# A five-stage gather kernel in which SyncE relays nothing: GpSimd waits for TensorE's count by a constant, VectorE for the landing of a fixed group

## The chip, the cores and the metric

The kernel runs on one core of a Trainium2 chip. The metric is the time of one execution on the device, in microseconds: before the change the median of three runs is 7366.6 us (7364.74 to 7367.6).

## What is computed

Four graph layers are applied to 6250 nodes of 256 features over 100,000 edges (`src`, `dst`; sorted by `dst`), each followed by a residual and a layer norm. What matters here is the sum over the edges that end in a node:

```
agg = jax.ops.segment_sum(h[src], dst, num_segments=n)              # layer 0
gathered = support[edge_col] * edge_val[:, None]                    # layer 1
out = jax.ops.segment_sum(msg, dst, num_segments=n_nodes)           # layer 2, three times
msg = jax.nn.relu(x[src] + edge_attr)                               # layer 3
agg = jax.ops.segment_sum(msg, dst, num_segments=x.shape[0])
```

The kernel does five of these sums by gathering rows by `src` and adding them up per `dst`: its gather stages 0 (layer 0), 2, 3, 4 (layer 2) and 5 (layer 3). Layer 1 is done in another way (a scatter with addition, between stages 0 and 2).

## The kernel before

**Blocks, tiles, pairs.** The sorted edges are cut into 782 blocks of 128, the nodes into 49 tiles of 128. A pair is a block and a tile that share an edge; there are about 830, padded to 832. Since both are sorted, pair p of tile t belongs to block p - t. Pairs are worked in 208 batches of four, blocks are gathered in 196 groups of four.

**A gather stage, engine by engine.**
- GpSimd (`gather`, line 466) issues one indirect DMA for each block: it brings the 128 source rows into one of the 64 slots of the buffer `ring`. The landing of group k is counted on the semaphore `gathered{k % 16}`. From group 16 on a group may start only when slots are free.
- VectorE (`one_hots`, line 1123) makes, for batch q, four 128 x 128 matrices that say which edge of the block ends in which node of the tile. Two batches fit the buffer `onehot`. It waits for the rows of the batch's last block, for the accumulator of its last tile (`cleared`), and for the first matmul of the batch before (`summed`).
- TensorE (`sum_pairs`, line 608) multiplies, four matmuls a batch, into one of four accumulators, and counts each pair on `summed{n}`. The count starts at 1.
- ScalarE (`sum_tiles`, line 870) takes a finished tile out of its accumulator.
- SyncE stands between them (`relay`). For each group it waits for the landing, adds the number of blocks to `landed{n}` (line 256), reads from the table `need` the last pair that uses group k - 4 (line 249), waits until `summed{n}` has reached it, and adds 1 to `freed` (line 251). GpSimd waits for `freed` before group k, which stands for group k - 16. So slots become free exactly when their last pair is done. VectorE waits for `landed{n}` against a number that it reads from the table `lasts`: exactly the last block that the batch uses.
- Stage 5 differs: GpSimd waits there for `summed5` against the constant `(k + 1) * BATCH - SLOTS + T`, and VectorE adds edge features to each landed group (`messages`, lines 1133 and 1134) right ahead of the one-hots of the batch with the same number.

**What else runs beside stage 0.** SyncE's relay of stage 0 also loads the tiles of `x` for a first matrix product (`y_step`), ten groups ahead of their use. VectorE compares shifted edge lists (`rows_of_edges`, lines 1218 and 1219) after each of the one-hots 1 to 127. Stage 0 starts before the tables of pairs are ready: GpSimd fills the ring, then waits.

Every engine works its own instructions in program order; a wait holds back all that stands behind it on that engine. After a stage all nodes must be summed before the next table can be written and the next stage's gathers can start.

Of the kernel before, what the change touches and what calls it, by code (L numbers as in the profile page):

```python
# [5 lines left out]
P = 128  # L6
ALU = mybir.AluOpType
ACT = mybir.ActivationFunctionType
ET = mybir.EngineType
# [6 lines left out]
BATCH = 4  # L16
SLOTS = 64
GROUPS = SLOTS // BATCH
ONEHOTS = 8
EAS = 8  # L20
BEHIND = 4
ZG = 13
Y0 = 40
YS = 2
# [8 lines left out]
def gnn_kernel(nc, a, out):  # L33
    N, D = a["x"].shape
    E = a["src"].shape[0]
    T = -(-N // P)
    LAST = N - (T - 1) * P
    NP = T * P
    DH = D // P
    W = D + 1  # L40
    B = -(-E // P)
# [3 lines left out]
    PAIRS = -(-(B + T) // (2 * BATCH)) * (2 * BATCH)  # L45
    HALF = PAIRS // 2
    QB = PAIRS // BATCH
    GB = -(-B // BATCH)
# [12 lines left out]
    with ExitStack() as ctx:  # L61
# [5 lines left out]
        def sm(name):  # L67
            if name not in sems:
                sems[name] = ctx.enter_context(nc.semaphore(name))
            return sems[name]  # L70
# [12 lines left out]
        lasts = {"dst": sb("lasts_dst", [1, QB * 2], U16)}  # L83
        need = {"dst": sb("need_dst", [1, 2 * P], U16)}
# [96 lines left out]
        y_rows_in = [bias[:, i, :] for i in range(3)] + [wt[w_][:, i, :] for w_ in "bd" for i in range(DH)]  # L181
        YB = len(y_rows_in)
        y_turned_in = [wt["c"][:, i, :] for i in range(DH)]

        def y_step(q, lag):
            t, r = divmod(q - Y0 - lag, YS)
            return t if r == 0 and 0 <= t < T else None
# [13 lines left out]
        def landing(n, k):  # L201

            n -= n > 1
            size = lambda kk: min(BATCH, B - kk * BATCH)
            g = k % GROUPS
            each = sum(size(kk) for kk in range(g, GB, GROUPS))
            return sm(f"gathered{g}"), 16 * (n * each + sum(size(kk) for kk in range(g, k + 1, GROUPS)))
# [6 lines left out]
        def before_stage(n):  # L214

            return n - (n > 1)
# [6 lines left out]
        def _(sp):  # L223
            def load(dst, src, sem):
                sp.dma_start(dst, src).then_inc(sem, 16)
# [17 lines left out]
            def weights(k, name):  # L243
                load(wt[k][:, :, :], a[name].rearrange("(h k) n -> k h n", k=P), sm("weights_in"))

            def free_slots(n, k):

                if 0 <= k < GB - GROUPS:
                    last_pair = sp.value_load(need[AGGS[n][0]][0:1, k:k + 1], min_val=1, max_val=PAIRS + 1)
                    sp.wait_ge(sm(f"summed{n}"), last_pair)  # L250
                    sp.sem_inc(sm("freed"), 1)

            def relay(n):
                for k in range(GB):
                    sp.wait_ge(*landing(n, k))
                    sp.sem_inc(sm(f"landed{n}"), min(BATCH, B - k * BATCH))
                    if k == BEHIND and n == 0:
                        sp.wait_ge(sm("tables_done"), n + 1)
                    free_slots(n, k - BEHIND)
                    t = y_step(k, -10) if n == 0 else None  # L260
                    if t is not None:
                        if t >= YB:
                            sp.wait_ge(sm("y_turned"), t - YB + 1)
                        elif t == 3 + DH:
                            sp.wait_ge(sm("w_turned"), 1)
                        if t >= 3:
                            sp.wait_ge(sm(f"x_in{t % 3}"), 16 * (t // 3))
                        rows_ = min(P, N - t * P)
                        load(y_rows_in[t % YB][0:rows_, :], a["x"][t * P:t * P + rows_, :], sm(f"x_in{t % 3}"))

            def store_table(name, src, ready, base=0):
                for t in range(T):
# [29 lines left out]
            for i, name in enumerate(("b1", "g1", "beta1", "br", "b2", "g2", "beta2")):  # L302
                columns(i, "L0_gnn_" + name)
            load(wt["d"][:, :, :], a["L0_gnn_w1"].rearrange("(h o) k -> o h k", o=P), sm("wnat_in"))
            relay(0)
            sp.wait_ge(sm("summed0"), PAIRS + 1)
            sp.wait_ge(sm("xr_free"), 1)
            for q, name in enumerate(("L0_gnn_w1", "L0_gnn_wr", "L0_gnn_wroot", "L0_gnn_w2")):
# [31 lines left out]
                    load(part[:, g % 2, j, 0:(t1 - t0) * D],  # L340
                         sums[j][0:NP, :].rearrange("(p t) d -> p (t d)", t=T)[:, t0 * D:t1 * D], sm(f"sums_in{g % 2}"))
            store_table("g0", lambda t: tile(H, t), sm("ln1_own"))
            relay(2)
            store_table("g1", lambda t: tile(H, t), sm("gcn_rows"))
            relay(3)
            store_table("g2", lambda t: tile(H, t), sm("gcn_rows"), T)
            sp.wait_ge(sm("gcn_rows"), 2 * T)
            for q, name in enumerate(("L3_gnn_W1", "L3_gnn_W2")):
# [2 lines left out]
                columns(i, "L3_gnn_" + name)  # L351
            for i, name in enumerate(("bn2_gamma", "bn2_beta", "bn2_mean", "bn2_var", "b2")):
                row(E1[:, i * D:(i + 1) * D], "L3_gnn_" + name, sm("bn2_in"))
            relay(4)
            store_table("x3", lambda t: tile(X, t), sm("ln2_rows"))

            disorder = sp.value_load(unsorted[0:1, 0:1], min_val=0, max_val=E)
# [27 lines left out]
        def _(pool):  # L385
# [61 lines left out]
            def gather(n, features=False):  # L447
                which, name = AGGS[n]
                if n > 2:
                    pool.wait_ge(sm(f"summed{n - 1}"), PAIRS + 1)  # L450
                for k in range(GB):
                    if k >= GROUPS:
                        if n < 5:
                            pool.wait_ge(sm("freed"), before_stage(n) * (GB - GROUPS) + k - GROUPS + 1)
                        else:
                            pool.wait_ge(sm(f"summed{n}"), (k + 1) * BATCH - SLOTS + T)
                    here = range(k * BATCH, min(B, (k + 1) * BATCH))
                    if features:
                        if k >= 2:
                            pool.wait_ge(sm("landed5"), (k - 1) * BATCH)  # L460
                        for b in here:
                            pool.indirect_dma_start(
                                out=EA[:, b % EAS, :], out_offset=None, in_=a["edge_attr_256"][:, :],
                                in_offset=bass.IndirectOffsetOnAxis(ap=eid[:, b:b + 1], axis=0)).then_inc(sm(f"ea_in{k % 2}"), 16)
                    for b in here:
                        pool.indirect_dma_start(  # L466
                            out=ring_v[:, b % SLOTS, 0:D], out_offset=None, in_=table[name][:, :],
                            in_offset=bass.IndirectOffsetOnAxis(ap=idx_ap[which][:, b:b + 1], axis=0))\
                            .then_inc(landing(n, k)[0], 16)
# [523 lines left out]
        def _(dve):  # L993
# [114 lines left out]
            def one_hots(n, q):  # L1108

                which = AGGS[n][0]  # L1110
                _, (block_end, tile_end_) = nc.values_load_multi_w_load_instructions(
                    lasts[which][0:1, 2 * q:2 * q + 2], engines=[ET.DVE], min_val=0, max_val=1023,
                    skip_runtime_bounds_check_because="made of clamped numbers")
                if q >= 2:
                    dve.wait_ge(sm(f"summed{n}"), (q - 1) * BATCH + 1)
                elif n > 2:
                    dve.wait_ge(sm(f"summed{n - 1}"), PAIRS + 1)
                elif n == 2:
                    dve.wait_ge(sm("c_mm"), QB)
                s = q * BATCH % ONEHOTS  # L1120
                dve.wait_ge(sm(f"landed{n}"), block_end)
                dve.wait_ge(sm(f"cleared{n}"), tile_end_)  # L1122
                last = tt(onehot[:, s:s + BATCH, :], iota_row[:, :].unsqueeze(1).to_broadcast((P, BATCH, P)),  # L1123
                          dl_ap[which][:, q * BATCH:(q + 1) * BATCH].unsqueeze(2).to_broadcast((P, BATCH, P)), ALU.is_equal)
                last.then_inc(sm("onehot_ready"), 1)
# [158 lines left out]
            for i in range(T + 2):  # L1284
# [4 lines left out]
                if i >= 2:  # L1289
                    t = i - 2  # L1290
# [237 lines left out]
```

## Time and profile before

| | |
|---|---|
| timed runs, median | 7366.6 us |
| profiled execution, span | 8074.1 us |
| TensorE matmul busy | 4409.3 us (55%) |
| VectorE busy | 2662.5 us (33%) |
| GpSimd busy | 5199.4 us (64%) |
| ScalarE busy | 866.9 us (11%) |
| indirect gathers | 3910 (782 a stage), 0.946 us each at the median |

The page is of one execution with the profiler on. Its span runs from the first to the last instruction, and the page records no time around it; it is 707.5 us longer than the median of the timed runs. "Busy" of GpSimd is here the issue of indirect DMAs. In the page's wait lists a releaser "remote" is one that the profile could not name, and "issue" is time in which an engine waited for nothing that the profile shows.

### The profile page before, as it was taken

Reading aid. Unit: us, or ns where it says so; the run is one execution under the profiler, and the core shown is the slowest. Engines: PE = TensorE matmul, PEld = TensorE weight load, DVE = VectorE, ACT = ScalarE, POOL = GpSimd, SP = SyncE. Lnnn points to the kernel's source line nnn. Section 1 sums busy time; section 2 is a strip of 40 time slices with the busy share of each in tenths; the row PEclk is TensorE's granted clock in tenths of the full one; section 3 lists DMA queues with packets and bytes.
Section 4 is the critical chain, followed back from the end, with each engine's and each line's share of the span. In section 5 each row is a group of like instructions: output and inputs, shape, how many; then the busy total and the mean of one; then the engine's idle time right before and its main releaser. Section 6 shows DMA issues by size and latency. Waiting matters only on the chain.

```text
span 8074.1 us, 63990 instructions
## 1 busy us (share of the span) xinstructions
PE 4409.3 (55%) x16498; PEld 3303.5 (41%) x16498; DVE 2662.5 (33%) x5948; ACT 866.9 (11%) x2041; POOL 5199.4 (64%) x4804
## 2 busy tenths in 40 slices
PE   3455559866666651444445444445544545556557
PEld 2344338755444440333334333334333334334336
DVE  5443212655555544111112111112111114544445
ACT  0000002322322220000002000002000001000002
POOL 4776660188888883666663666663666663677774
PEclk9777779988888875777777677667777667766768
DMA  2333334166666665333332333333333333666662
GB/s 64 95 104 103 97 90 136 19 72 71 72 72 72 71 72 177 89 91 94 91 94 86 87 93 93 92 93 94 88 93 93 92 91 101 185 182 185 184 182 64
DMA packets 497711, 811.01 MB, mean 100 GB/s; under 512 B 97410, under 2 KB 367636, under 8 KB 497364
## 3 DMA queue, kind: packets, MB, share of 16 engines
q0 software_dynamic: 300288, 615.29, 34.2%
q1 hardware_dynamic: 197076, 191.58, 7.4%
q8 instruction: 159, 2.61, 0.1%
q14 instruction: 188, 1.54, 0.1%
HBM read 652.63 MB, written 153.86 MB: 100 GB/s over the span
## 4 chain that ended last, share of the span: by engine, by line
another core or an unknown queue 28%; PE 25%; POOL 20%; issue 17%; DVE 6%; DMA 2%; DVEq 1%; SPq 0%; ACT 0%; POOLq 0%; ACTq 0%
PE acc L608 17%; POOL sums_by_src L488 11%; POOL ring L466 9%; DVE onehot L1123 3%; PE acc L532 3%; PE acc L527 2%; PE high L527 1%; DVEq L1122 1%; DVE X L1154 1%; PE high L518 1%; DMA ring<-table_x,idx_dst 1%; DMA sums_by_src<-ring,E 1%; PE high L532 1%; PE acc L518 0%
## 5 line engine op out<-in xcount | busy, mean ns | idle before, releaser
L608 PE MATMUL acc<-ring,onehot 128*128 x8320 | 2738.6, 490 | 2828.7 <-DVE onehot L1123 1780.1
L608 PEld LDWEIGHTS acc<-ring,onehot 128*128 128x128 f32 x8320 | 1958.4, 246 | 3581.4 <-issue 3237.5
L466 POOL DMA_INDIRECT ring<-table_g,idx_dst x2346 | 2290.3, 976 | 1338.0 <-issue 683.5
L1123 DVE TENSOR_TENSOR onehot<-iota_row,dl_dst 128x512 f32<-128x512 f32 x1040 | 720.3, 694 | 3556.4 <-remote 2262.8
L488 POOL DMA_INDIRECT sums_by_src<-ring,E x782 | 1208.1, 1545 | 613.0 <-ACT high L925 373.9
L466 POOL DMA_INDIRECT ring<-table_x,idx_dst x782 | 833.1, 1065 | 418.8 <-issue 343.1
L466 POOL DMA_INDIRECT ring<-in_x_dram,idx_dst x782 | 792.2, 1013 | 407.8 <-issue 243.3
L768 PE MATMUL high<-H,ring 128*128 x1664 | 546.1, 485 | 455.3 <-ACT high L925 441.6
L768 PEld LDWEIGHTS high<-H,ring 128*128 128x128 f32 x1664 | 375.3, 236 | 550.7 <-issue 490.0
L870 ACT COPY H<-acc 128x256 f32<-128x256 f32 x196 | 72.9, 372 | 4461.8 <-PE acc L608 2781.7
L1365 DVE TENSOR_SCALAR ring<-acc,E 128x128 f32<-128x128 f32 x832 | 283.7, 402 | 575.9 <-PE acc L536 575.9
L1133 DVE TENSOR_TENSOR ring<-ring,E 128x1024 f32<-128x1024 f32 x196 | 239.8, 1223 | 507.3 <-DMA ring<-table_x,idx_dst 476.9
L939 ACT COPY ring<-high 128x512 f32<-128x512 f32 x392 | 210.4, 589 | 1005.6 <-DMA sums_by_src<-ring,E 979.0
L536 PEld LDWEIGHTS acc<-ring,onehot 128*128 128x128 f32 x1664 | 240.0, 207 | 137.7 <-issue 133.6
L536 PE MATMUL acc<-ring,ones 128*128 128x512 f32 x416 | 271.8, 742 | 2.3 <-DVE ring L1353 2.3
L1353 DVE TENSOR_SCALAR ring<-ident,E,ones 128x128 f32<-128x128 f32 x832 | 244.2, 386 | 0.0
L1361 DVE TENSOR_SCALAR onehot<-iota_row,dl_dst,ones 128x128 f32<-128x128 f32 x832 | 234.2, 355 | 0.0
L536 PE MATMUL acc<-ring,onehot 128*128 128x128 f32 x1664 | 232.1, 285 | 2.4 <-DVE ring L1365 2.4
L925 ACT ACTIVATE high<-ones 128x512 f32<-128x512 f32 x396 | 221.1, 591 | 6.2
L527 PE MATMUL high<-wt_c,wt_a 128*128 128x128 f32 x392 | 72.1, 343 | 189.0 <-issue 189.0
L527 PEld LDWEIGHTS high<-wt_c,wt_a 128*128 128x128 f32 x392 | 66.4, 249 | 202.0 <-issue 200.2
L1134 DVE TENSOR_SCALAR ring<-ring 128x1024 f32<-128x1024 f32 x196 | 136.0, 694 | 21.2 <-DVE ring L1133 0.5
(259 smaller groups left out, 2914.9 us busy)
## 6 DMA issues: line engine op xcount, KB each, us to landing
E<-in_edge_attr_dram SPq DMA_DIRECT2D x781, 128.0 KB
ring<-table_g,idx_dst POOLq DMA_INDIRECT x2346
table_g<-H SPq DMA_DIRECT2D x147, 128.0 KB, 1.7
ring<-sums_by_src SPq DMA_DIRECT2D x36, 512.0 KB, 4.8
sums_by_src<-ring SPq DMA_DIRECT2D x2, 6272.0 KB, 38.8
ring<-in_x_dram,idx_dst POOLq DMA_INDIRECT x782
sums_by_src<-ring,E POOLq DMA_INDIRECT x782, 3.8
ring<-table_x,idx_dst POOLq DMA_INDIRECT x782
```

The lines of the kernel that those rows point to most:

```text
L466: pool.indirect_dma_start(out=ring_v[:, b % SLOTS, 0:D], out_offset=None, in_=table[name][:, :], in_offset=bass.IndirectOffsetOnAxis(ap=id ...
L488: pool.indirect_dma_start(out=sums[j][:, :], out_offset=bass.IndirectOffsetOnAxis(ap=to_b[:, b:b + 1], axis=0), in_=rows[:, b % (4 * BATCH ...
L527: last = pe.matmul(chunk(to, o), wk, val, start=(i == 0), stop=(i == len(steps) - 1))
L532: last = pe.matmul(to[:, 0:D], chunk(val, k), wk[:, k, :], start=(k == 0), stop=(k == DH - 1))
L536: return pe.matmul(to, w_, v, start=start, stop=stop, skip_group_check=True)
L608: pe.matmul(acc4[:, ds(to, width)], onehot[:, (q * BATCH + j) % ONEHOTS, :], ring[:, ds(slot, width)], start=False, stop=True, skip_group_ ...
L768: last = pe.matmul(high[:, ds(to, D)], cT[:, (k * BATCH + j) % ONEHOTS, :], H[:, ds(at, D)], start=False, stop=True, skip_group_check=True)
L1123: last = tt(onehot[:, s:s + BATCH, :], iota_row[:, :].unsqueeze(1).to_broadcast((P, BATCH, P)), dl_ap[which][:, q * BATCH:(q + 1) * BATCH] ...
L1133: link(tt(g, g, EA[:, at:at + here, :], ALU.add))
L1353: last = ts(diag[:, p % ONEHOTS, :], ident[:, :], src_q[:, p:p + 1], ones[:, 0:1], ALU.mult, ALU.mult)
L1361: ts(onehot[:, p % ONEHOTS, :], iota_row[:, :], dl["dst"][:, p:p + 1], ones[:, 0:1], ALU.is_equal, ALU.mult)
L1365: last = ts(eqw[:, p % ONEHOTS, :], bank[k % 2][:, j * P:(j + 1) * P], src_q[:, p:p + 1], w_q[:, p:p + 1], ALU.is_equal, ALU.mult)
```

## The change

SyncE's `relay` and `free_slots` are gone from all stages. In stage 0 SyncE only loads the tiles of `x`, one after another, as their buffers come free. GpSimd waits in stages 0, 2, 3 and 4 as it does in stage 5: for TensorE's own count, against a constant. VectorE waits for its batch q in those stages for the landing of the whole group q (none for batches 196 to 207, since there is no such group), and reads one number from its table instead of two. Stage 5 stays as it was.

```
-            def free_slots(n, k):
-                if 0 <= k < GB - GROUPS:
-                    last_pair = sp.value_load(need[AGGS[n][0]][0:1, k:k + 1], min_val=1, max_val=PAIRS + 1)
-                    sp.wait_ge(sm(f"summed{n}"), last_pair)
-                    sp.sem_inc(sm("freed"), 1)
-
-            def relay(n):
-                for k in range(GB):
-                    sp.wait_ge(*landing(n, k))
-                    sp.sem_inc(sm(f"landed{n}"), min(BATCH, B - k * BATCH))
-                    if k == BEHIND and n == 0:
-                        sp.wait_ge(sm("tables_done"), n + 1)
-                    free_slots(n, k - BEHIND)
-                    t = y_step(k, -10) if n == 0 else None
-                    if t is not None:
...
+            def x_for_first_pass():
+                for t in range(T):
+                    if t >= YB:
+                        sp.wait_ge(sm("y_turned"), t - YB + 1)
+                    elif t == 3 + DH:
+                        sp.wait_ge(sm("w_turned"), 1)
+                    if t >= 3:
+                        sp.wait_ge(sm(f"x_in{t % 3}"), 16 * (t // 3))
...
-            relay(0)
+            x_for_first_pass()
...
-            relay(2)
...
-            relay(3)
...
-            relay(4)
...
                     if k >= GROUPS:
-                        if n < 5:
-                            pool.wait_ge(sm("freed"), before_stage(n) * (GB - GROUPS) + k - GROUPS + 1)
-                        else:
-                            pool.wait_ge(sm(f"summed{n}"), (k + 1) * BATCH - SLOTS + T)
+                        pool.wait_ge(sm(f"summed{n}"), (k + 1) * BATCH - SLOTS + T)
...
-                _, (block_end, tile_end_) = nc.values_load_multi_w_load_instructions(
-                    lasts[which][0:1, 2 * q:2 * q + 2], engines=[ET.DVE], min_val=0, max_val=1023,
+                first_word = 2 * q if n == 5 else 2 * q + 1
+                _, ends = nc.values_load_multi_w_load_instructions(
+                    lasts[which][0:1, first_word:2 * q + 2], engines=[ET.DVE], min_val=0, max_val=1023,
...
-                dve.wait_ge(sm(f"landed{n}"), block_end)
-                dve.wait_ge(sm(f"cleared{n}"), tile_end_)
+                if n == 5:
+                    dve.wait_ge(sm("landed5"), ends[0])
+                elif q < GB:
+                    dve.wait_ge(*landing(n, q))
+                dve.wait_ge(sm(f"cleared{n}"), ends[-1])
```

No instruction of GpSimd, VectorE or TensorE moves past another; what changes is what they wait for. On GpSimd, at the start of stage 0, the rows of before and then of the changed kernel (the 64 gathers that fill the ring, then group 16 and the first gather of group 17; `freed` is SyncE's count, `summed0` TensorE's):

```order
L466 DMA ring<-in_x_dram,idx_dst 128x256 [waits edges_ready,idx_ready]
L466 DMA ring<-in_x_dram,idx_dst 128x256 x63
L466 DMA ring<-in_x_dram,idx_dst 128x256 [waits freed]
L466 DMA ring<-in_x_dram,idx_dst 128x256 x3
L466 DMA ring<-in_x_dram,idx_dst 128x256 [waits freed]
```

```order
L445 DMA ring<-in_x_dram,idx_dst 128x256 [waits edges_ready,idx_ready]
L445 DMA ring<-in_x_dram,idx_dst 128x256 x63
L445 DMA ring<-in_x_dram,idx_dst 128x256 [waits summed0]
L445 DMA ring<-in_x_dram,idx_dst 128x256 x3
L445 DMA ring<-in_x_dram,idx_dst 128x256 [waits summed0]
```

The gathers stand where they stood; the wait for `freed` has become one for `summed0`, for group 16 for the value 17 * 4 - 64 + 49 = 53.

On VectorE, near the end of stage 2, batches 193 to 195 of before and then 193 to 197 of the changed kernel (`gathered1` to `gathered3` are the landings of groups 193 to 195):

```order
L1123 TENSOR_TENSOR onehot<-iota_row,dl_dst 128x512 [waits cleared2,landed2,summed2]
L1111 TENSOR_LOAD lasts_dst
L1123 TENSOR_TENSOR onehot<-iota_row,dl_dst 128x512 [waits cleared2,landed2,summed2]
L1111 TENSOR_LOAD lasts_dst
L1123 TENSOR_TENSOR onehot<-iota_row,dl_dst 128x512 [waits cleared2,landed2,summed2]
```

```order
L1106 TENSOR_TENSOR onehot<-iota_row,dl_dst 128x512 [waits cleared2,gathered1,summed2]
L1091 TENSOR_LOAD lasts_dst
L1106 TENSOR_TENSOR onehot<-iota_row,dl_dst 128x512 [waits cleared2,gathered2,summed2]
L1091 TENSOR_LOAD lasts_dst
L1106 TENSOR_TENSOR onehot<-iota_row,dl_dst 128x512 [waits cleared2,gathered3,summed2]
L1091 TENSOR_LOAD lasts_dst
L1106 TENSOR_TENSOR onehot<-iota_row,dl_dst 128x512 [waits cleared2,summed2]
L1091 TENSOR_LOAD lasts_dst
L1106 TENSOR_TENSOR onehot<-iota_row,dl_dst 128x512 [waits cleared2,summed2]
```

The wait for SyncE's `landed2` has become one for the landing of the group with the batch's own number, and from batch 196 on (the last two rows) there is none.

## Rows read from the trace of the kernel before

**Rows 1.** The page: span, busy time of each engine, the costliest gather group.
```profile
span 8074.1 us, 63990 instructions
PE 4409.3 (55%) x16498; PEld 3303.5 (41%) x16498; DVE 2662.5 (33%) x5948; ACT 866.9 (11%) x2041; POOL 5199.4 (64%) x4804
L466 POOL DMA_INDIRECT ring<-table_g,idx_dst x2346 | 2290.3, 976 | 1338.0 <-issue 683.5
```
**Rows 2.** Windows of the gather instructions, first to last, stages 0, 2 and 5.
```profile
core 0: us, POOL busy (x), PEclk, DMA share, GB/s
19.90:1204.60 1184.70, 792.20 (x782) 0.79 0.32 92
3130.80:4243.00 1112.20, 765.76 (x782) 0.70 0.32 92
...
6773.80:7905.90 1132.10, 833.13 (x782) 0.68 0.63 181
```
**Rows 3.** Timeline of VectorE, start of stage 2.
```profile
3137.59 0.69 DVE L1123 TENSOR_TENSOR onehot<-iota_row,dl_dst 128x512 f32<-128x512 f32 x1 [8.94 <-SPq L256]
3142.54 0.69 DVE L1123 TENSOR_TENSOR onehot<-iota_row,dl_dst 128x512 f32<-128x512 f32 x1 [4.26 <-issue]
...
3187.31 0.69 DVE L1123 TENSOR_TENSOR onehot<-iota_row,dl_dst 128x512 f32<-128x512 f32 x1 [21.06 <-remote]
3209.01 0.69 DVE L1123 TENSOR_TENSOR onehot<-iota_row,dl_dst 128x512 f32<-128x512 f32 x1 [21.01 <-remote]
```
**Rows 4.** Timeline of GpSimd, start of stage 2: last gather of group 0.
```profile
3134.70 0.95 POOL L466 DMA_INDIRECT ring<-table_g,idx_dst  x1 [0.30 <-issue]
```
**Rows 5.** SyncE's instructions of line 249, 3160 to 3235 us, then 166 to 215.
```profile
L249 SPq FUSED_REGOPS  x6: 691/701/717, 3164.1 to 3216.7; - x6
...
L249 SPq FUSED_REGOPS  x14: 147/147/147, 166.6 to 212.7; - x14
```
**Rows 6.** Timeline of TensorE, 3186 to 3232 us.
```profile
3188.15 3.78 PE L608 MATMUL acc<-ring,onehot 128*128 x8 [18.22 <-DVE onehot L1123]
```
**Rows 7.** GpSimd's waits: stage 2, then stage 5.
```profile
POOL ring L466 <- SPq L251: 118.2, 37, 12.9
...
POOL ring L466 <- remote: 48.4, 29, 3.2
POOL ring L466 <- PE acc L608: 27.3, 19, 21.7
```
**Rows 8.** Windows of the one-hots, from last gather's end to last matmul.
```profile
1204.60:1237.40 32.80, 8.28 (x12) 1.00 0.02 5
4243.00:4281.20 38.20, 9.68 (x14) 0.98 0.02 4
...
7905.90:7943.40 37.50, 9.67 (x14) 0.98 0.02 6
```
**Rows 9.** Timeline of VectorE, end of stage 2.
```profile
4258.32 0.69 DVE L1123 TENSOR_TENSOR onehot<-iota_row,dl_dst 128x512 f32<-128x512 f32 x1 [1.85 <-PE acc L608]
...
4276.13 0.69 DVE L1123 TENSOR_TENSOR onehot<-iota_row,dl_dst 128x512 f32<-128x512 f32 x1 [1.99 <-PE acc L608]
```
**Rows 10.** Timeline of TensorE, end of stage 2.
```profile
4253.75 1.99 PE L608 MATMUL acc<-ring,onehot 128*128 x8 [0.52 <-issue]
```
**Rows 11.** Timeline of GpSimd, start of stage 0.
```profile
166.40 1.65 POOL L466 DMA_INDIRECT ring<-in_x_dram,idx_dst  x1 [66.60 <-SPq L251]
...
204.99 1.65 POOL L466 DMA_INDIRECT ring<-in_x_dram,idx_dst  x1 [0.30 <-issue]
```
**Rows 12.** Timeline of VectorE, start of stage 0.
```profile
163.24 0.69 DVE L1123 TENSOR_TENSOR onehot<-iota_row,dl_dst 128x512 f32<-128x512 f32 x1 [6.09 <-ACT acc L887]
...
201.47 1.01 DVE L1219 TENSOR_TENSOR H<-H 128x819 f32<-128x819 f32 x1
203.18 0.69 DVE L1123 TENSOR_TENSOR onehot<-iota_row,dl_dst 128x512 f32<-128x512 f32 x1 [0.69 <-PE acc L608]
```
**Rows 13.** Timeline of TensorE beside it.
```profile
204.02 2.00 PE L608 MATMUL acc<-ring,onehot 128*128 x8 [1.35 <-DVE onehot L1123]
```

More of the change, by code:

```diff
@@ L20 @@
 EAS = 8
-BEHIND = 4
 ZG = 13
@@ L244, in weights @@
                 load(wt[k][:, :, :], a[name].rearrange("(h k) n -> k h n", k=P), sm("weights_in"))
-            def free_slots(n, k):
-                if 0 <= k < GB - GROUPS:
-                    last_pair = sp.value_load(need[AGGS[n][0]][0:1, k:k + 1], min_val=1, max_val=PAIRS + 1)
-                    sp.wait_ge(sm(f"summed{n}"), last_pair)
-                    sp.sem_inc(sm("freed"), 1)
-            def relay(n):
-                for k in range(GB):
-                    sp.wait_ge(*landing(n, k))
-                    sp.sem_inc(sm(f"landed{n}"), min(BATCH, B - k * BATCH))
-                    if k == BEHIND and n == 0:
-                        sp.wait_ge(sm("tables_done"), n + 1)
-                    free_slots(n, k - BEHIND)
-                    t = y_step(k, -10) if n == 0 else None
-                    if t is not None:
[L262 to L269, printed above, removed]
+            def x_for_first_pass():
[6 more added lines that the diff above has]
+                        sp.wait_ge(sm(f"x_in{t % 3}"), 16 * (t // 3))
+                    rows_ = min(P, N - t * P)
+                    load(y_rows_in[t % YB][0:rows_, :], a["x"][t * P:t * P + rows_, :], sm(f"x_in{t % 3}"))
             def store_table(name, src, ready, base=0):
```

## The prediction

> **What bounds the kernel now.** I read the page first, then the windows of the five gather stages, then the timelines at the start and the end of a stage, and last the waits. The page shows no engine near full: GpSimd 64%, TensorE 55% [rows 1]. So the bound has to be read stage by stage. In the windows of the gather instructions each stage lasts 1110 to 1185 us and GpSimd issues 782 gathers in it [rows 2]. At the start of stage 2, before anything is late, the gathers take 0.95 us and 0.30 us of issue lie between two [rows 4], so a gather costs 1.25 us and a group of four 5.0 us, and VectorE makes one batch of one-hots every 4.95 us (3137.59, 3142.54), right after each landing [rows 3]. There GpSimd's issue is the bound and the others follow. A batch costs TensorE 1.99 us and 0.52 us between two [rows 10], 2.51 us, when nothing is missing: half of what a group costs GpSimd.
>
> Twenty microseconds later the picture is another one. One-hots come every 21.7 us [rows 3], a batch of eight matmul records that the trace models with 3.78 us is followed by 18 us of nothing [rows 6], and SyncE's small register instruction takes 0.701 us where it takes 0.147 us elsewhere [rows 5]. The consumers fall behind until the ring is full, and GpSimd waits 118.2 us in stage 2 for slots [rows 7]. The question on which the forecast hangs is whether the timed runs have these stretches. The profiled span is 8074.1 us [rows 1], the median of the timed runs 7366.6 us: 707.5 us less. Take the stretches away and the stages at 782 x 1.25 = 977 us each: stages 2, 3, 4 (3 and 4 are like 2, within 2 us) and 5 lose 3 x 134 + 155 = 557 us [rows 2]; stage 0 runs from 166.4 us [rows 11] to 1204.6 with 718 gathers, 898 us, and is left with 140, of which (792.2 / 782 - 0.95) x 782 = 49 us is longer gathers that may stay, so it loses 91; and the ends of stage, 33 to 38 us [rows 8], shrink in the four stages before the last to about 6 (below), 4 x 29 = 116. That is 764 us to be had in these places, of which 707.5 are missing from the timed runs. No other stage has idle time of this kind in such an amount. I take it that the timed runs have next to none of it: GpSimd's issue is the bound of all five gather stages, and the rest follows close behind.
>
> A rule of the Trainium skill speaks for this reading ("NOTIFIC — the notification-queue block", section "7.1 Overflow: three behaviours, one of which stalls the engine"): the block that writes an engine's profile records holds the engine back rather than lose a record inside itself. By that rule the stretches belong to the profiled execution, and the sum would be the +147 us below; were they real, it would be the first rival's. No run here shows the block itself.
>
> **The change part by part.** All sums start from the median, 7366.6 us, since the terms are taken from stretches of the profiled execution (8074.1 us, nothing recorded around it) that the disturbance does not touch.
>
> (a) End of stages 0, 2, 3, 4. Pair p of tile t uses block p - t. Batch q ends with pair 4q + 3, and at the end of a stage t is 48, so before the change batch 206 needs block 779 (group 194) and only batch 207 needs group 195. When the last group lands, one batch is open. After the change batch 195 waits for group 195, so batches 195 to 207 are open, thirteen. Twelve batches more, at TensorE's 2.51 us each (VectorE: 4276.13 - 4258.32 = 17.81 us for seven, 2.54) [rows 9, 10]: 30.1 us a stage, 120.5 us in four. Nothing covers it: the next table can't be written before all is summed. Stage 5 already has this form, and its end takes 37.5 us for 14 one-hots [rows 8]. The short end that I take for before is 3137.59 - 3135.65 = 1.9 us for the landing [rows 3, 4], 0.69 for the one-hots, some 0.9 to the matmul (204.02 - 203.18 plus, as in stage 0) and 2.0: about 6 us. Bounds: 1.99 us a batch if the gap is the profiler's (96 us in four stages), and 3.78 + 0.52 = 4.3 us a batch at TensorE's lower clock level, as in [rows 6] (206 us). The ends shown ran at a granted clock of 0.98 to 1.00 [rows 8], so I take 2.51.
>
> (b) Start of stage 0. The ring is full and all landed when the tables are ready. Before, GpSimd goes on after batch 0, at 166.40 us [rows 11]. After, it waits for 53 on `summed0`, which begins at 1: for 52 pairs, batches 0 to 12. The one-hots of batch 12 start at 203.18 us, and its matmuls end at 206.0 [rows 12, 13]. In these 40 us GpSimd has issued 24 gathers (the rows from 166.40 to 204.99, of 1.08 and 1.65 to 1.79 us in turn beside VectorE's comparisons of edges, one of them in rows 12) [rows 11]. After the change these 24 are issued later, at 1.25 us: 30 us more. The comparisons of batches 13 to 127 lie beside gathers in both kernels and cancel. VectorE reads one number for two ahead of each of the 13 batches; its 0.69 us of idle time there [rows 12] may fall by a quarter of a microsecond, 3 us in all. Together +27. Bounds: 22 and 40.
>
> (c) The steady part. GpSimd's gather k asks for all batches up to k - 4, and batch k - 4 can start when group k - 4 has landed. From the start of group k - 4: 5.0 us of issue, 1.9 landing, 0.7 one-hots, 0.9, and 2.0 to 3.8 of matmul, 10.5 to 12.3 us; in stage 0 up to 2 us of comparisons more. GpSimd comes to group k at 20 us. So nothing waits, and the change costs 0; the cover is 6 to 8 us. It is gone if something holds a batch for longer. VectorE's one long piece in stage 0 (after batch 128) may cost a few us once. If the cover were always as thin as in the disturbed stage 5, GpSimd would wait 48.4 + 27.3 = 76 us a stage [rows 7]; that is the upper bound, 303 us in four. Below zero it can't go in the undisturbed case, since GpSimd issues without a pause already.
>
> (d) What is removed. SyncE's relay is out of the chain from landing to one-hots: 0.1 us once a stage, nothing. SyncE has no other work in stages 2 to 4, and its loads of x in stage 0 come as early as before or earlier.
>
> Sum: 120.5 + 27 + 0 = 147; 7366.6 + 147 = 7514 us, 2.0% slower.
>
> **The rivals.**
> First rival, faster: the stretches are real, and with them the consumers' lag. Then the ends are already 33 to 38 us with twelve to fourteen one-hots open [rows 8], and (a) is 0. The waits for slots, 118.2 us in stage 2, fall to the 76 us of stage 5's constant [rows 7], or further if SyncE's polling is what makes them: 4 x 42 = 169 us gained, 27 lost, 7225 us. For it: rows 8 as they stand, and that the stretch in stage 2 begins when SyncE starts on `need`. Against it: the 707.5 us, and stage 0's SyncE rows, 0.147 us with the same work [rows 5]. It decides if, without a profiler, more than about eight batches are open at the last gather. 0.10.
>
> Second rival, slower still: the cover of (c) is too thin, or the ends run at the lower clock level. (a) at 4.3 us a batch gives 206 + 27, 7600 us; half of (c)'s bound would give 7666. Against it: the clock in rows 8, and the 20 us against 12. 0.11.
>
> Third rival, little happens: the lag is real in part, so that (a) costs a third or less and only the start of stage 0 remains: 7366.6 + 27 + 0 to 40 = 7394 to 7434. 0.09, of which 0.02 within 0.2% if a small gain in waiting meets the 27 us.
>
> **How the numbers follow.** The forecast, (a) at 1.99 to 2.9 us a batch and (b) at 22 to 40, gives 7485 to 7546, and with a few us of stalls 7480 to 7560; chance 0.70. To hold 8 in 10 the range takes in part of the third rival below and of the second above: 7435 to 7580. A measurement of this kernel tells a difference of 0.2%, 15 us. Faster 0.10, within 0.2% 0.02, slower 0.88.
>
> **What would show it.** In the changed profile: (a) 13 one-hots after each stage's last gather, as before, and, since the disturbance may still be there, the sign in the page may differ from the timed one; the tell is the difference of span and timed median, which should be smaller than 707.5 by the ends and the waits for slots. (b) The first gather after the full ring at 203 to 207 us, not 166.4. (c) GpSimd's waits released by TensorE at line 445: short ones only. The prediction is wrong if the timed runs have a lag that the undisturbed stretches of this trace don't show, or if the next stage's work starts on something else than the last sum.

## The result, and the profile after

The changed kernel takes 7494.97 us, the median of four runs (7486.86 to 7504.56); beside it on the same chip the kernel before took 7367.1 us (7364.74 to 7367.62). The ratio is 1.0172, with a 95% interval of 1.016 to 1.0185: 127.9 us slower, 147 were forecast.

The profiled span tells the opposite at first sight, 7484.8 us against the 8074.1 of [rows 1]. So the kernel before was profiled once more, unchanged. The page of the changed kernel, and then that of this second profile of before:

```profile
span 7484.8 us, 60326 instructions
PE 4617.8 (62%) x16498; PEld 3373.7 (45%) x16498; DVE 2664.6 (36%) x5948; ACT 866.9 (12%) x2041; POOL 5088.7 (68%) x4804
L445 POOL DMA_INDIRECT ring<-table_g,idx_dst x2346 | 2219.7, 946 | 1007.0 <-issue 688.5
```

```profile
span 7366.0 us, 63990 instructions
PE 4590.6 (62%) x16498; PEld 3371.5 (46%) x16498; DVE 2662.6 (36%) x5948; ACT 866.9 (12%) x2041; POOL 5121.4 (70%) x4804
```

The second profile has the same 63990 instructions and a span within 3 us of the timed runs. The 708 us of the first belonged to that one profiled execution, and from here on the second stands for before. The two spans now differ by 118.8 us. Each is of one execution, and the changed kernel's profiled one took 7486.86 us, the shortest of its four. So the timed 127.9 us is the better number, and the traces say where the 118.8 sit; the other 9 us are in no trace.

The windows of the gathers in the changed kernel, one row for each gather stage (0, 2, 3, 4, 5), from the first gather's start to the last one's end:

```profile
20.50:1089.20 1068.70, 763.37 (x782) 0.83 0.36 102
3014.00:3992.40 978.40, 740.45 (x782) 0.77 0.37 105
4086.30:5063.70 977.40, 739.49 (x782) 0.77 0.36 105
5158.40:6136.00 977.60, 739.67 (x782) 0.76 0.37 106
6256.60:7316.40 1059.80, 821.79 (x782) 0.69 0.67 194
```

And of the kernel before, second profile:

```profile
20.00:1069.90 1049.90, 781.73 (x782) 0.84 0.37 104
2971.20:3953.00 981.80, 743.90 (x782) 0.77 0.37 105
4016.60:4998.60 982.00, 744.08 (x782) 0.77 0.37 105
5064.10:6046.80 982.70, 744.75 (x782) 0.77 0.37 106
6136.70:7198.00 1061.30, 823.32 (x782) 0.70 0.67 193
```

Stages 2 to 4, which were 1111 to 1112 us, are 982 to 983: GpSimd issues without a pause in both kernels. What stands out is the gaps between rows. In the changed kernel the next stage starts later after the last gather. The windows of the one-hots from the last gather's end to the last matmul, stages 0, 2, 3, 4, in the changed kernel and then in the one before:

```profile
1089.20:1124.90 35.70, 9.06 (x14) 0.95 0.02 4
3992.40:4028.40 36.00, 8.95 (x14) 1.00 0.02 4
5063.70:5099.50 35.80, 9.08 (x14) 1.00 0.02 4
6136.00:6172.20 36.20, 9.32 (x14) 1.00 0.02 5
```

```profile
1069.90:1076.80 6.90, 0.79 (x2) 0.55 0.09 20
3953.00:3958.70 5.70, 0.86 (x2) 0.70 0.09 25
4998.60:5005.50 6.90, 0.82 (x2) 0.54 0.10 22
6046.80:6052.30 5.50, 0.79 (x2) 1.00 0.10 25
```

(A window counts an instruction that it only touches: of the 14 and the 2, 13 and 1 start after the last gather.) These are the two columns to subtract:

| us, after minus before | stage 0 | 2 | 3 | 4 | 5 |
|---|---|---|---|---|---|
| end, last gather to last matmul | +28.8 | +30.3 | +28.9 | +30.7 | 0 |
| window of the gathers | +18.8 | -3.4 | -4.6 | -5.1 | -1.5 |

The ends sum to +118.7, the windows of the gathers to +4.2; the stretches between the stages account for the -4.1 that is left to the 118.8 of the spans.

What an end is made of, VectorE's timeline at the end of stage 2 in the changed kernel:

```profile
3991.76 0.69 DVE L1106 TENSOR_TENSOR onehot<-iota_row,dl_dst 128x512 f32<-128x512 f32 x1 [4.31 <-DMA ring<-table_g,idx_dst]
3995.09 1.29 DVE L1106 TENSOR_TENSOR onehot<-iota_row,dl_dst 128x512 f32<-128x512 f32 x2 [2.64 <-DMA ring<-table_g,idx_dst]
3997.96 0.69 DVE L1106 TENSOR_TENSOR onehot<-iota_row,dl_dst 128x512 f32<-128x512 f32 x1 [1.58 <-PE acc L587]
...
4023.33 0.69 DVE L1106 TENSOR_TENSOR onehot<-iota_row,dl_dst 128x512 f32<-128x512 f32 x1 [1.82 <-PE acc L587]
```

The same place in the kernel before, from the timeline of all engines, the last gather and the last one-hots:

```profile
3952.05 0.94 POOL L466 DMA_INDIRECT ring<-table_g,idx_dst  x1 [0.30 <-issue]
...
3955.44 0.69 DVE L1123 TENSOR_TENSOR onehot<-iota_row,dl_dst 128x512 f32<-128x512 f32 x1 [2.27 <-SPq L256]
```

Before, one batch follows the last landing. After, the two that start at 3995.09 are batch 195, which was held for group 195, and batch 196 behind it; TensorE then paces the other eleven, from 3997.96 to 4023.33, 2.54 us apart and released by `PE acc`. That makes thirteen. (The section on the kernel before says that VectorE waits for the first matmul of the batch before. By the code, `(q - 1) * BATCH + 1` on a count that begins at 1, it waits for the last matmul of the batch two before, whose place in `onehot` it takes. That is why two can start at once.)

The start of stage 0, GpSimd's timeline, changed kernel and then before:

```profile
100.34 0.95 POOL L445 DMA_INDIRECT ring<-in_x_dram,idx_dst  x1 [0.30 <-issue]
168.97 0.94 POOL L445 DMA_INDIRECT ring<-in_x_dram,idx_dst  x1 [67.68 <-PE acc L587]
```

```profile
100.07 0.95 POOL L466 DMA_INDIRECT ring<-in_x_dram,idx_dst  x1 [0.30 <-issue]
131.52 1.65 POOL L466 DMA_INDIRECT ring<-in_x_dram,idx_dst  x1 [30.50 <-SPq L251]
```

With the ring full, GpSimd goes on 37.2 us later after its last gather (67.68 against 30.50). Before, this is at 131.52 us for the 166.40 of [rows 11]: those 35 us belonged to the disturbed execution too.

Between start and end nothing waits. The waits of GpSimd in the changed kernel, stage 2 alone and then from the first gather after the full ring to the end of stage 0 (us in total, times, longest):

```profile
POOL ring L445 <- PE acc L587: 7.9, 26, 0.3
```

```profile
POOL ring L445 <- PE acc L587: 18.3, 60, 0.3
```

0.3 us is what lies between any two gathers. No wait on TensorE's count is longer, where the disturbed execution waited 118.2 us for SyncE's count in stage 2 [rows 7].

### The profile page after: what moved, and what is told of

It reads as the page before. It is cut to its first block, busy times and chain, and to the rows that moved or that the text cites. A ratio compares the mean times of both kernels' runs of the same rounds, so it can differ in the third digit from the quotient of the medians.

```text
span 7484.8 us, 60326 instructions
## 1 busy us (share of the span) xinstructions
PE 4617.8 (62%) x16498; PEld 3373.7 (45%) x16498; DVE 2664.6 (36%) x5948; ACT 866.9 (12%) x2041; POOL 5088.7 (68%) x4804
## 4 chain that ended last, share of the span: by engine, by line
POOL 51%; issue 21%; PE 15%; DMA 7%; DVE 6%; SPq 0%; DVEq 0%; ACT 0%; POOLq 0%; ACTq 0%
POOL ring L445 39%; POOL sums_by_src L467 12%; PE acc L587 7%; PE acc L511 3%; DMA ring<-table_g,idx_dst 3%; PE acc L506 2%; DVE onehot L1106 2%; DMA ring<-in_x_dram,idx_dst 2%; DMA ring<-table_x,idx_dst 1%; DVE X L1137 1%; PE high L506 1%; DVE H L991 1%; DMA sums_by_src<-ring,E 1%; PE high L511 1%; PE high L497 1%
## 5 line engine op out<-in xcount | busy, mean ns | idle before, releaser
L587 PE MATMUL acc<-ring,onehot 128*128 x8320 | 2957.2, 517 | 2250.9 <-DVE onehot L1106 2218.1
L587 PEld LDWEIGHTS acc<-ring,onehot 128*128 128x128 f32 x8320 | 2030.0, 256 | 3147.0 <-issue 2783.5
L445 POOL DMA_INDIRECT ring<-table_g,idx_dst x2346 | 2219.7, 946 | 1007.0 <-issue 688.5
L445 POOL DMA_INDIRECT ring<-in_x_dram,idx_dst x782 | 763.4, 976 | 321.3 <-issue 235.3
L515 PEld LDWEIGHTS acc<-ring,onehot 128*128 128x128 f32 x1664 | 239.1, 206 | 137.8 <-issue 134.3
L1357 DVE COPY ring<-acc 128x512 f32<-128x512 f32 x208 | 141.2, 679 | 1.6 <-PE acc L515 1.6
L849 ACT COPY X<-acc 128x256 f32<-128x256 f32 x49 | 18.2, 372 | 955.0 <-PE acc L587 955.0
```

The lines of the kernel that those rows point to most:

```text
L445: pool.indirect_dma_start(out=ring_v[:, b % SLOTS, 0:D], out_offset=None, in_=table[name][:, :], in_offset=bass.IndirectOffsetOnAxis(ap=id ...
L515: return pe.matmul(to, w_, v, start=start, stop=stop, skip_group_check=True)
L587: pe.matmul(acc4[:, ds(to, width)], onehot[:, (q * BATCH + j) % ONEHOTS, :], ring[:, ds(slot, width)], start=False, stop=True, skip_group_ ...
```

## The experiments

All seven are of one core and timed against the kernel before on the same chip, which took 7361.3 us beside the first four and 7362.0 beside the others. The diffs are against the changed kernel, except where one says otherwise.

**One half of the change at a time.** The first kernel keeps SyncE's relay of landings (and VectorE's exact last block) and changes only what GpSimd waits for:

```
+            def relay(n):
+                for k in range(GB):
+                    sp.wait_ge(*landing(n, k))
+                    sp.sem_inc(sm(f"landed{n}"), min(BATCH, B - k * BATCH))
...
-                if n == 5:
-                    dve.wait_ge(sm("landed5"), ends[0])
-                elif q < GB:
-                    dve.wait_ge(*landing(n, q))
+                dve.wait_ge(sm(f"landed{n}"), block_end)
```

> The changed kernel, but SyncE relays the landings again and VectorE waits for the last block that its batch uses; GpSimd keeps TensorE's count by the constant. My theory (the loss is open batches at four ends of stage, about 100 to 120 us, and the later start of gathers after the full ring in stage 0, about 27 us): the ends are short again, the late start stays, so 27 us above before, 7394 us, ratio 1.0037. Rival (GpSimd's constant holds it back all along the stages): 7480 us or more, since that constant stays. Rival (the first one of the prediction, consumers lag whatever they wait for): no change against the changed kernel, 7495 us.

Measured: 7387.06 us (7385.84 to 7406.74, six runs), ratio 1.0037 (1.0024 to 1.0049), 25.7 us. GpSimd's timeline behind the full ring:

```profile
173.55 0.95 POOL L453 DMA_INDIRECT ring<-in_x_dram,idx_dst  x1 [72.39 <-PE acc L595]
```

The start is late as in the changed kernel, and the four ends are 5.7 to 5.9 us. The constant of GpSimd alone costs the start of stage 0; nothing more is seen.

The second kernel is the other half: SyncE reads `need` and frees slots exactly, VectorE waits for the whole group q.

```
+                for k in range(GB):
+                    sp.wait_ge(*landing(n, k))
...
+                    free_slots(n, k - BEHIND)
...
-                        pool.wait_ge(sm(f"summed{n}"), (k + 1) * BATCH - SLOTS + T)
+                        if n < 5:
+                            pool.wait_ge(sm("freed"), before_stage(n) * (GB - GROUPS) + k - GROUPS + 1)
+                        else:
+                            pool.wait_ge(sm(f"summed{n}"), (k + 1) * BATCH - SLOTS + T)
```

> The other half: SyncE frees the slots exactly for GpSimd again, VectorE waits for the landing of the whole group with its batch's number. My theory: the start of stage 0 is as before, the four long ends stay, 100 to 120 us above before, 7467 to 7487 us, ratio 1.014 to 1.016. Rival (GpSimd's constant is the loss): 7367 us. If the profiled execution of this kernel is again some hundreds of us longer than its timed runs and that of the run above is not, then SyncE's reading of the table and its wait against a register go with the disturbance; if both are long, SyncE's relaying as such does.

Measured: 7462.64 us (7454.43 to 7474.76, four runs), ratio 1.0133 (1.0117 to 1.0148), 101.3 us: 4 us under the range expected. GpSimd's timeline and its waits:

```profile
131.92 1.43 POOL L465 DMA_INDIRECT ring<-in_x_dram,idx_dst  x1 [30.85 <-SPq L251]
```

```profile
POOL ring L465 <- SPq L251: 35.7, 17, 30.8
```

The start is the early one, the four ends are 35.8 to 35.9 us. The windows of its gathers, stages 0 and 2 (3 and 4 are 979.6 and 980.3 us long):

```profile
20.20:1062.30 1042.10, 773.45 (x782) 0.84 0.36 105
2993.70:3973.30 979.60, 741.46 (x782) 0.77 0.36 105
```

The halves add up: 25.7 + 101.3 = 127.0 us, and the whole change measured 127.9. The intervals reach some 9 to 12 us to either side of each, and within them neither half is seen to change what the other costs. Neither half has the long stretches in its profile: the spans are 7404.6 and 7472.7 us.

**The ends repaired without SyncE.** If the ends cost because batch q waits for group q, a nearer group must give the time back, with no relay at all. The third kernel works the group out from the batch's last pair and a lower bound on its tile, which rises by one each 17 pairs. The bound fits these evenly spread edges; with others the number of a tile can lag more, and the wait would be too early.

```
+            def group_of(q):
+                p = q * BATCH + BATCH - 1
+                return min(GB - 1, (p - max(0, p * T // (B + T) - 1)) // BATCH)
...
-                elif q < GB:
-                    dve.wait_ge(*landing(n, q))
+                else:
+                    dve.wait_ge(*landing(n, group_of(q)))
```

> The changed kernel without any relay, but VectorE's batch q waits for the landing of the group that holds its last block by the arithmetic of sorted edges (pair p of tile t uses block p - t, with t at least 49 p / 831 - 1), at the end of a stage twelve batches ahead of the changed kernel. The bound on t is fitted to edges spread evenly like these and is not safe for others. My theory: the four ends are short, the late start of stage 0 stays: 7394 us, ratio 1.0037, as in the run with the relayed landings, with one batch after each stage's last landing in the profile. Rival (it is the absence of SyncE that costs): 7495 us.

Measured: 7388.34 us (7379.47 to 7402.68, six runs), ratio 1.0033 (1.002 to 1.0045), 27.0 us, the same as the first kernel. The ends are 7.7 to 8.7 us, with two one-hots after the last gather, not the one expected: by the bound both batch 206 and batch 207 wait for group 195.

The fourth does the like for GpSimd's wait in stage 0 as well, where the constant T = 49 is replaced by an estimate of the tiles passed so far, which again fits these edges only:

```
+                        by_slots = (k + 1) * BATCH - SLOTS
+                        passed = by_slots + by_slots * T // B + 2
-                        pool.wait_ge(sm(f"summed{n}"), (k + 1) * BATCH - SLOTS + T)
+                        pool.wait_ge(sm(f"summed{n}"), min(passed, by_slots + T) if n == 0 else by_slots + T)
```

> As the run before it, and in stage 0 GpSimd waits for the pairs that pass a group by the same arithmetic, so group 16 may start after 6 pairs and not after 52. My theory: both terms gone, equal to before, 7367 us, ratio 0.998 to 1.002; the difference to the run before it is the start of stage 0, 27 us. If it is clearly below before, the relay had a cost of its own.

Measured: 7360.85 us (7350.94 to 7366.87, eleven runs) against 7361.33, ratio 0.9997 (0.9988 to 1.0006). The first value that GpSimd waits for is 6, on a count that begins at 1, so five pairs, not the six expected. GpSimd behind the full ring:

```profile
134.57 1.37 POOL L447 DMA_INDIRECT ring<-in_x_dram,idx_dst  x1 [33.44 <-PE acc L589]
```

SyncE has no part in this kernel's gathers either, and it takes the time of before. So the removal of the relay is worth nothing that the interval of -9 to +4 us lets one see, and the two coarser waits are the whole cost. In the traces two small differences make up this equality: the four ends are 7 us longer in all than before, the four windows of gathers 11 us shorter. No kernel here beats the one before by more than a measurement tells.

**How far the steady part is from the edge.** The last two put the landing that VectorE waits for one and two groups later, to measure the cover of 6 to 8 us that the prediction gave the steady part.

```
-                    dve.wait_ge(*landing(n, q))
+                    dve.wait_ge(*landing(n, min(q + 1, GB - 1)))
```

> The changed kernel, but in stages 0, 2, 3 and 4 VectorE's batch q waits for the landing of group q + 1 (the last one for batch 195). My theory: one more batch is open at each end of stage, 4 x 2.5 = 10 us, and GpSimd still never waits, since batch k - 4 is done some 15 us (5.0 more of issue than before) after the start of its group and GpSimd comes to group k 20 us after it: 7367 + 128 + 10 = 7505 us, ratio 1.0187. Rival (the cover between TensorE and GpSimd is already used up, a part of the 128 us): each group would be late by up to 5 us more, 7700 us and above.

Measured: 7501.29 us (7496.07 to 7504.97, five runs), ratio 1.0187 (1.0174 to 1.0201). The ends are 38.2 to 38.6 us, one batch longer, and the stages 2 to 4 stay at 977.6 to 978.3 us: a group of 5 us of delay in every batch costs only the one batch at each end, 11.4 us in time (139.3 us above its kernel before, for 127.9).

```
-                    dve.wait_ge(*landing(n, q))
+                    dve.wait_ge(*landing(n, min(q + 2, GB - 1)))
```

> As the run before it with group q + 2. Now batch k - 4 starts 6.7 us after the start of group k - 2 and is done 9.6 us after it at TensorE's higher clock level and 11.4 at the lower one, and GpSimd comes to group k after 10.0 us. My theory: two batches more a stage, 20 us, and stalls of up to 1.4 us a group where the clock is low (mean granted 0.8), half of 4 x 180 groups: 7515 to 8000 us, I expect 7700, ratio 1.045. If it is 7515, the cover is larger than I took it to be; if it is far over 8000, smaller, and then the one of the changed kernel is thin.

Measured: 7998.81 us (7997.98 to 8004.4, five runs), ratio 1.0866 (1.0851 to 1.0881). The direction was expected, not the size: the number given was 7700, and the time falls at the very end of the range. The waits of GpSimd in the kernel with one group more and then with two:

```profile
POOL ring L445 <- PE acc L587: 119.9, 166, 67.8
```

```profile
POOL ring L445 <- PE acc L587: 662.8, 567, 69.3
```

The timeline in stage 2 with two groups more:

```profile
3502.25 0.95 POOL L445 DMA_INDIRECT ring<-table_g,idx_dst  x1 [0.30 <-issue]
3503.84 0.95 POOL L445 DMA_INDIRECT ring<-table_g,idx_dst  x1 [0.65 <-PE acc L587]
...
3505.97 3.78 PE L587 MATMUL acc<-ring,onehot 128*128 x8 [2.40 <-DVE onehot L1106]
...
3510.01 0.94 POOL L445 DMA_INDIRECT ring<-table_g,idx_dst  x1 [1.48 <-PE acc L587]
...
3515.28 0.94 POOL L445 DMA_INDIRECT ring<-table_g,idx_dst  x1 [0.55 <-PE acc L587]
```

Here GpSimd stops at the first gather of two groups in three, until TensorE has counted a batch that it could not start earlier: of the 720 groups that need freed slots in these four stages, 461 wait for longer than 0.35 us. The waits are 543 us more in all, in 401 more of them. Each holds the 0.30 us that lie between any two gathers anyhow, so 421 us are added. Another 65 us are longer gathers, since the one-hots now fall across the starts of gathers (60 or 61 a stage over 1.0 us, 2 to 5 with one group more), and 12 us are longer ends. That makes 498, and the time rises by 497.5 us. The number given beforehand had the waits too small (7700 - 7515 = 185 us), had no longer gathers, and took the mean granted clock at 0.8, where the whole run had 0.737. The windows of stage 2 with one group more and then with two:

```profile
3024.20:4002.50 978.30, 740.35 (x782) 0.76 0.37 105
3145.30:4243.90 1098.60, 758.40 (x782) 0.65 0.33 94
```

The clock fell with the waits, from 0.76 to 0.65 in stage 2. Whether it lengthened them is not shown. The cover is thus more than 5 us (one group costs nothing) and less than 10 (two groups cost in most groups), which holds the 6 to 8 us. An estimate from the windows: they are 120 us longer over the 180 groups that need freed slots, 1.3 us for two groups. So from the start of group k - 2 to the end of batch k - 4, which waits for that group, pass 11.3 us at most on average, and the cover, 20 less this, is nearer 9 than 6.

**The kernel before once more**, profiled, with no edit:

> The kernel before, unchanged, profiled once more. The profiles of the two halves (relayed landings alone, freed slots alone) show stages of 980 us, a span close to the timed runs and one batch open at the end with exact waits. My theory: the long stretches in the first profile come with the profiler, not with the kernel's timed runs; whether this one has them again tells only how often. If it has a span near 7365 us, its ends of stage are 6 us long and its gathers have 12 to 14 lengthened ones a stage, as in the run with relayed landings. If it is again 8000 us or more, then the profiler and both jobs of the relay together bring them about.

Measured: span 7366.0 us, time 7368.05. Its rows are those shown above as before: the ends are 5.5 to 6.9 us, and 19, 13 and 18 gathers take over 1.0 us in stages 2, 3 and 4. What set the disturbance off, and whether the profiler had a part in it, stays open.

## Why the prediction was right, and where it was off

**The bound (GpSimd's issue, no lag in the timed runs).** Right, and it was the assumption on which the sign hung. It was drawn from the difference of 707.5 us between the first profile's span and the timed median; the second profile shows stages 2 to 4 at 982 us (977 forecast) and one open batch at the last gather. The sum of 764 us behind it was right in the whole and off in two parts. Between the two profiles stage 5 lost 71 us for the 155, since its gathers take 1.05 us each (823.32 / 782) in the undisturbed execution too, and stage 0 lost 135 for the 91; with 387 in stages 2 to 4 and 117 at the ends it is 710. The block of the Trainium skill's page "NOTIFIC — the notification-queue block" (section "7.1 Overflow: three behaviours, one of which stalls the engine") that can hold an engine back is not shown by any run; what is shown is that the stretches belonged to one execution, since the other profiles, taken with a profiler on as well, have none.

**The first rival (faster, 7225 us)** had rows 8 for it, twelve to fourteen one-hots open before the change. The second profile has one. **The third (7394 to 7434)** falls by the ends of 36 us. **The second (7600 to 7666)** falls by the clock in the windows of the ends, 0.95 to 1.00, which is the level of 2.4 GHz, and by waits of 0.3 us.

**(a) The ends: the term whose size was off.** Its own number holds: twelve batches more at 2.51 us were to be 30.1 us, and the four ends grew by 28.8 to 30.7, with the short end at 5.5 to 6.9 us for the 6 forecast. But it took that as the cost, 120.5 us in four, where the second experiment measured 101.3. The step that failed is that it counted only where the twelve batches go and gave nothing back where they come from. Stage 3 of before and then of after, all gathers (duration ns min/median/max):

```profile
L466 POOL DMA_INDIRECT ring<-table_g,idx_dst x782: 942/946/1402, 4016.6 to 4997.7; - x196
```

```profile
L445 POOL DMA_INDIRECT ring<-table_g,idx_dst x782: 942/946/1056, 4086.3 to 5062.8; - x196
```

The median is one and the same, the longest is not. There are 208 batches for 196 groups, so before the change two batches follow one landing about every sixteenth group. The timeline of before at one such place:

```profile
4178.65 1.37 DVE L1123 TENSOR_TENSOR onehot<-iota_row,dl_dst 128x512 f32<-128x512 f32 x2 [4.45 <-SPq L256]
4179.44 1.40 POOL L466 DMA_INDIRECT ring<-table_g,idx_dst  x1 [0.30 <-issue]
```

Two one-hots in a row, and the gather that starts beside the second takes 1.40 us instead of 0.95. In stage 3 of before thirteen gathers take over 1.0 us, most of them some 80 us apart (4099.1, 4179.4, 4259.9 and so on), after the change one. Another of the thirteen:

```profile
4098.19 1.37 DVE L1123 TENSOR_TENSOR onehot<-iota_row,dl_dst 128x512 f32<-128x512 f32 x2 [4.31 <-SPq L256]
4099.15 1.23 POOL L466 DMA_INDIRECT ring<-table_g,idx_dst  x1 [0.30 <-issue]
```

In both places the gather ends 0.82 us after the second one-hots (4180.84 - 4180.02 and 4100.38 - 4099.56), however much of it was left at the gather's start.

GpSimd is busy for 744.08 us in stage 3 before and 739.49 after, 4.6 us less, and that is the 4.6 us by which the window is shorter. The long gathers account for it: what those over 1.0 us take beyond 0.946 each is 4.1, 4.7 and 5.4 us in stages 2, 3 and 4 before, and 0.8, 0.1 and 0.3 after, against windows that are 3.4, 4.6 and 5.1 us shorter. The experiments agree. Where two batches can follow one landing (before, the first, third and fourth kernels), 10 to 19 gathers take over 1.0 us in each of the stages 2 to 4; where batch q waits for group q or q + 1 (the changed kernel, the second and the fifth), 1 to 5 do.

How much is given back in all is known less well. In the second experiment's trace the windows of stages 0, 2, 3 and 4 are 7.8 + 2.2 + 2.4 + 2.4 = 14.8 us shorter and the ends 118.3 us longer, 103.5 together, for the 101.3 timed. With the changed kernel's windows for stages 2 to 4 it would be 21 us. Either is most of the 19 us that were forecast too many, of which 2 are the ends themselves (118.7 for 120.5). A window is good to 2 or 3 us: stage 5, the same in all kernels, is 2.4 us longer in the second experiment's trace, and the third and fourth kernels have the same waits in stage 2 and windows of 982.7 and 979.9 us. Of the 7.8 us of stage 0, 5.4 are gathers that started beside one-hots; the rest are gathers beside the comparisons of edges, and why those fall better is not shown.

**(b) The start: right, for a partly other place.** 27 us forecast; 25.7 by the first experiment, and 27.5 by the third less the fourth (7388.34 - 7360.85). GpSimd goes on 37.2 us later for the 40 forecast. In the windows of stage 0 this shows as +18.8 only, because it is met by the 7.8 us less of (a): 1068.7 - 1042.1 = 26.6 against the second experiment. The forecast named 203 to 207 us for the first gather and it came at 168.97: the time of the tables was read from the disturbed execution. The distance was read there too, and held. The 3 us taken off for the shorter read of the table may be more: the first experiment, which reads two numbers and waits for the relayed count, goes on after 72.39 us, the changed kernel and the third, with one number, after 67.68 and 68.16.

**(c) The steady part: right.** 0 forecast, and no wait above 0.3 us. The cover of 6 to 8 us lies between the 5 us that cost nothing and the 10 us that cost 497.5; the estimate above puts it nearer 9.

**(d) The relay: right.** The fourth kernel has none and takes 7360.85 us for 7361.33. Here a go-between costs nothing that can be measured, while GpSimd's issue is the bound and what SyncE adds is inside the cover.

Sum as measured: 101.3 + 25.7 + 0 + 0 = 127.0, for 120.5 + 27 + 0 + 0. Each term was of the right kind and in the right place. Only (a) was mis-sized, by what its step left out.

## What to carry to other kernels

A wait that is made coarser (a constant for a count that was read, a whole group for a last block) costs nothing in the steady part as long as its cover is longer than the delay; look for its price where there is no next piece of work to hide it, at the start of a stage with a full buffer and at the end with an empty queue, and count that price once for each stage where it arises. Work that moves to the end also leaves the place that it came from; ask what it slowed there. In both places a bound that can be worked out beforehand did as well as an exact number that an engine had to relay, for these evenly spread edges; for others such a bound would have to be proved. And hold the span of a profile against the timed median before a row of it is used: where they differ by 10%, find the stretches in which they do and forecast from the others, or take a second profile.

## What the runs showed of the hardware

- One profiled execution can be unlike all others of the same program: 8074.1 and 7366.0 us for the same 63990 instructions. The disturbed one had one-hots 21.7 us apart and SyncE's register instructions at 0.701 us for 0.147 in stretches [rows 3, 5]; none of the eight other profiles of this study has such an instruction of over 0.5 us.
- The issue of a gather is held by a comparison of VectorE that is already running, and not by one that starts after it. In stages 2 to 4 of the eight undisturbed traces 336 gathers start while a one-hots comparison has 0.20 to 0.67 us left, and every one of them ends 0.81 to 0.83 us after the comparison does, so they take 1.02 to 1.48 us. Of the 4508 gathers within which such a comparison starts, none takes over 0.96 us. Where the two start within 0.04 us of each other (11 gathers), the gather keeps its 0.94 to 0.95 us and the comparison takes 0.72 to 0.76 us instead of 0.69. One of the 4508, in the changed kernel:

```profile
3190.62 0.94 POOL L445 DMA_INDIRECT ring<-table_g,idx_dst  x1 [0.30 <-issue]
3190.95 0.69 DVE L1106 TENSOR_TENSOR onehot<-iota_row,dl_dst 128x512 f32<-128x512 f32 x1 [3.95 <-issue]
```

  The Trainium skill's page "SBUF — State Buffer" (section "Who interferes with whom") says that a VectorE instruction with both inputs in that memory contends with a GpSimd instruction that reads it; the row at 4179.44 agrees, if a gather, whose row names the indices `idx_dst` as an input, is such an instruction. The same section reports that `tensor_tensor`, the operation of these one-hots, was not seen to stall a DMA; for the issue of these gathers the measurement says otherwise.
- The edge of the cover is sharp: 5 us more of delay in each batch cost 11.4 us in the whole kernel (139.3 above the kernel before for 127.9), the next 5 us cost 497.5.
